# A recommendation model on one core: one gathered column of seven tiles moves from GpSimd to row-by-row DMAs of SyncE

## The reference

```python
h = relu(dense @ dw1 + db1)
dense_emb = relu(h @ dw2 + db2)
sparse_emb = emb_tables[f_ids, sparse_idx]
emb = concatenate([dense_emb[:, None, :], sparse_emb], axis=1)   # 27 vectors of 64
inter = einsum('bfd,bgd->bfg', emb, emb)
pairs = inter[:, iu0, iu1]                                       # 351 products
z = concatenate([emb.reshape(B, -1), pairs], axis=1)
z = relu(z @ ow1 + ob1); z = relu(z @ ow2 + ob2); z = relu(z @ ow3 + ob3)
return z @ ow4 + ob4
```

## Time and profile before

| what | value |
|---|---|
| median of 3 runs | 552.72 us (552.71 to 553.63) |
| profiled execution, its own time | 554.64 us |
| span of the profiled execution | 552.7 us |
| mean granted TensorE clock | 0.928 of full speed |
| busy: PE, POOL | 444.2 us (80%), 398.2 us (72%) |
| busy: ACT, DVE | 159.4 us (29%), 141.9 us (26%) |
| DMA traffic | 19.38 MB, mean 35 GB/s |

### The profile page before, as it was taken

One profiled execution on the slowest core, in us unless ns is written; L12 is line 12 of the kernel. 1 busy time (PEld: TensorE's weight loads), 2 busy tenths in 40 slices (PEclk: granted clock), 3 DMA queues, 4 the chain that ended last, 5 costly groups with the idle time before them and its releaser, 6 DMA issues.

```text
span 552.7 us, 5884 instructions
## 1 busy us (share of the span) xinstructions
PE 444.2 (80%) x2326; PEld 236.6 (43%) x2326; DVE 141.9 (26%) x225; ACT 159.4 (29%) x265; POOL 398.2 (72%) x420
## 2 busy tenths in 40 slices
PE   3757989585887979799685988979597899959978
PEld 1124553252534435354342534525253444525767
DVE  1003324031331223214032231413222123311412
ACT  1303334122232232324133232323333223332322
POOL 5777777777777777777777777777777777777720
PEclk9999999798898979979798998979989799997998
DMA  8633323233332323333232332324333232333310
GB/s 274 133 49 25 29 26 25 27 28 26 27 26 26 27 26 28 26 27 26 26 28 26 27 26 28 27 26 27 26 28 26 26 27 26 27 25 27 26 13 1
DMA packets 17166, 19.38 MB, mean 35 GB/s; under 512 B 7359, under 2 KB 8386, under 8 KB 17127
## 3 DMA queue, kind: packets, MB, share of 16 engines
q0 software_dynamic: 13312, 13.66, 30.5%
q1 hardware_dynamic: 3408, 5.02, 2.7%
q10 hardware_dynamic: 420, 0.34, 0.3%
HBM read 18.99 MB, written 0.01 MB: 34 GB/s over the span
## 4 chain that ended last, share of the span: by engine, by line
POOL 57%; issue 19%; PE 15%; DMA 6%; SPq 1%; ACT 1%; DVE 1%; POOLq 0%; DVEq 0%
POOL emb L212 57%; DMA w1p_sb<-ow_pairs_dram 5%; PE l_ps L588 5%; PE gram_ps L567 2%; PE tr_ps L616 2%; PE l_ps L656 1%; DMA emb<-table_dram,rows 1%; PE gram_ps L656 1%; PE tr_ps L540 1%; PE l_ps L594 1%; PE gram_ps L635 0%; SPq L189 0%; PE l_ps L581 0%; PE gram_ps L663 0%; PE l_ps L663 0%
## 5 line engine op out<-in xcount | busy, mean ns | idle before, releaser
L212 POOL DMA_INDIRECT emb<-table_dram,rows x416 | 398.0, 957 | 130.1 <-issue 125.6
L588 PE MATMUL l_ps<-w_sb,feat 128*128 128x512 f32 x390 | 204.3, 674 | 3.7 <-DVE feat L247 1.5
L588 PEld LDWEIGHTS l_ps<-w_sb,feat 128*128 128x128 f32 x390 | 81.8, 220 | 107.6 <-issue 89.8
L540 PE MATMUL tr_ps<-ident_sb,emb 128*128 128x128 f32 x208 | 39.3, 306 | 62.5 <-DMA emb<-table_dram,rows 61.4
L278 DVE COPY gram_c<-gram_ps 32x432 f32<-32x432 f32 x60 | 36.6, 610 | 138.8 <-PE gram_ps L567 138.4
L382 ACT COPY slots<-feat 64x512 f32<-64x512 f32 (+3 forms) x66 | 58.6, 888 | 45.6 <-DVE feat L247 43.6
L567 PEld LDWEIGHTS gram_ps<-slots 64*128 64x128 f32 x960 | 56.1, 188 | 26.8 <-issue 15.5
L567 PE MATMUL gram_ps<-slots 64*128 64x108 f32 x960 | 61.2, 277 | 6.7 <-DVE gram_c L278 6.7
L394 ACT COPY gram_c<-gram_ps 32x432 f32<-32x432 f32 x60 | 30.6, 509 | 122.4 <-PE gram_ps L567 122.0
L247 DVE COPY feat<-tr_ps 128x512 f32<-128x512 f32 (+1 forms) x32 | 15.7, 492 | 191.4 <-PE tr_ps L540 191.4
L540 PEld LDWEIGHTS tr_ps<-ident_sb,emb 128*128 128x128 f32 x208 | 26.1, 152 | 90.2 <-issue 88.7
(11 more groups left out here) (67 smaller groups left out, 174.9 us busy)
## 6 DMA issues: line engine op xcount, KB each, us to landing
emb<-table_dram,rows POOLq DMA_INDIRECT x416, 3.3
w_sb<-ow_dram SPq DMA_DIRECT2D x3, 1024.0 KB, 9.7
w1p_sb<-ow_pairs_dram SPq DMA_DIRECT2D x1, 708.0 KB
w_sb<-ow_dram SPq DMA_DIRECT2D x1, 512.0 KB, 21.8
w_sb<-ow_dram SPq DMA_DIRECT2D x1, 256.0 KB, 13.0
idx_raw<-idx_dram ACTq DMA_DIRECT2D x1, 208.0 KB, 2.6
w1d_sb<-ow_dram SPq DMA_DIRECT2D x1, 128.0 KB
w_sb<-ow_dram SPq DMA_DIRECT2D x1, 128.0 KB, 6.4
```

The lines of the kernel that those rows point to most:

```text
L212: pool.indirect_dma_start(out=emb[:, t % RING, c // 2, c % 2 * D:(c % 2 + 1) * D], out_offset=None, in_=table, in_offset=bass.IndirectOffs ...
L540: last = nc.tensor.transpose(tr_ps[:, n % 2, (k - a) * P:(k - a + 1) * P], emb[:, t % RING, k, :], ident_sb[:])
L588: nc.tensor.matmul(l1_ps[t % 2][:], feat[t % 2][:, n - 1, :], w1_sb[:, n - 1, :], start=False, stop=False)
```

## The change

In tiles 2, 4, 6, 8, 10, 12 and 15 the last column (the odd half of pair 12, the last one of the fourth group) is left out of POOL's loop. SP fetches it in its place: 128 DMAs a tile, one for each sample, each of one row of 256 bytes to one partition. The row numbers of these columns come in a small array of their own, one partition wide; ACT's queue loads it, three DVE instructions turn it into row numbers. SP reads 32 of them at a time into registers and issues 32 DMAs whose source address is worked out from a register. For a tile t of 4 or more it first waits until PE has transposed all of tile t-4. PE's wait ahead of the fourth group is lowered by 16 for each column that POOL no longer fetches, and a wait for the tile's own 128 row DMAs is added. SP's six stores of the result now stand behind all the row DMAs in its program.

```diff
+ROW_TILES = [2, 4, 6, 8, 10, 12, 15]
+ROWS_AT_ONCE = 32
...
+        row_raw = sb("row_raw", [1, len(ROW_TILES), P], I32)
+        row_wrap = sb("row_wrap", [1, len(ROW_TILES), P])
+        row_f = sb("row_f", [1, len(ROW_TILES), P])
+        row_of = sb("row_of", [1, len(ROW_TILES), P], I32)
...
             sp.dma_start(w4_sb[:], ow4).then_inc(w234_in, 16)
 
+            sp.wait_ge(row_step, 3)
+            for i, t in enumerate(ROW_TILES):
+                if t >= RING:
+                    sp.wait_ge(transposed, (t - RING + 1) * NG)
+                for p in range(0, P, ROWS_AT_ONCE):
+                    _, r = nc.values_load_multi_w_load_instructions(
+                        row_of[0:1, i, p:p + ROWS_AT_ONCE], engines=[mybir.EngineType.SP], min_val=0,
+                        max_val=NF * V - 1, skip_runtime_bounds_check_because="DVE clamps every row number")
+                    for k in range(ROWS_AT_ONCE):
+                        sp.dma_start(emb[p + k:p + k + 1, t % RING, NP - 1, D:2 * D],
+                                     table[bass.ds(r[k], 1), :]).then_inc(row_gathered[i], 16)
+
             for b, (a, e) in enumerate(BATCHES):
...
-                    for c in range(2 * a, 2 * b):
+                    for c in range(2 * a, 2 * b - (b == NP and t in ROW_TILES)):
                         pool.indirect_dma_start(
...
+            dve.wait_ge(row_idx_in, 16)
+            nc.vector.tensor_scalar(row_wrap[:], row_raw[:], 0.0, float(V), ALU.is_lt, ALU.mult).then_inc(row_step, 1)
+            dve.wait_ge(row_step, 1)
+            nc.vector.scalar_tensor_tensor(out=row_f[:], in0=row_raw[:], scalar=float(-V), in1=row_wrap[:],
+                                           op0=ALU.max, op1=ALU.add).then_inc(row_step, 1)
+            dve.wait_ge(row_step, 2)
+            nc.vector.tensor_scalar(row_of[:], row_f[:], float(V - 1), float((NF - 1) * V),
+                                    ALU.min, ALU.add).then_inc(row_step, 1)
...
             act.dma_start(idx_raw[:], idx).then_inc(idx_in, 16)
+            act.dma_start(row_raw[:], row_idx).then_inc(row_idx_in, 16)
             act.dma_start(bias_sb[:], biases).then_inc(dense_w_in, 16)
...
-                pe.wait_ge(gathered[t % RING][n], (t // RING + 1) * 32 * (b - a))
+                by_row = [u for u in ROW_TILES if u % RING == t % RING and u <= t and b == NP]
+                pe.wait_ge(gathered[t % RING][n], (t // RING + 1) * 32 * (b - a) - 16 * len(by_row))
+                if t in by_row:
+                    pe.wait_ge(row_gathered[ROW_TILES.index(t)], 16 * P)
```

More of the change, by code:

```diff
@@ L27, in bass_dlrm_kernel @@
     first: bass.AP,
+    row_idx: bass.AP,
     table: bass.AP,
@@ L119, in bass_dlrm_kernel @@
         gathered = [[sem(f"gathered{r}_{n}") for n in range(NG)] for r in range(RING)]
+        row_gathered = [sem(f"row_gathered{i}") for i in range(len(ROW_TILES))]
+        row_idx_in = sem("row_idx_in")
+        row_step = sem("row_step")
         out_stored = sem("out_stored")
@@ L783 @@
         "first_dram": _np.stack([base, idx[:, 0]], axis=1),
+        "row_idx_dram": _np.stack([idx[:, t, NF - 1] for t in ROW_TILES])[None],
         "table_dram": x["emb_tables"].reshape(NF * V, D),
```

## The result

The changed kernel takes **546.92 us** (median of 4 runs, 545.59 to 547.17). The kernel before took 553.17 us (4 runs, 552.71 to 553.96). The ratio is 0.9878, with a 95% interval of 0.9858 to 0.9899: 1.2% faster. The forecast was 545.1 us, 1.4% faster; against the 552.72 us that it started from that is a ratio of 0.9862, just inside the interval.

What follows compares the result with a forecast made beforehand. POOL's gathers, 1.262 us each, were taken as the bound until PE's tail; six fewer gave 552.7 - 7.6 = 545.1 us. The likeliest case spanned 543.5 to 547; the wider range reached up to 590.

Steps and rivals of the forecast that it cites:

- POOL as the bound, 1.262 us a gather, six that count: POOL's gather loop: six of seven dropped gathers lie ahead of the chain's last one, saving 7.6 us.
- The seventh: Tile 15's dropped gather, the very last of the kernel, where PE is not waiting: saves nothing.
- The cost of a row: SP's row loop: DMA 0.278 us with its pause, two short instructions, register load 0.075 a row; 0.45 us in all.
- The upper bound of 0.88: SP's cost per row at most 0.88 us, charging POOL's 0.30 us pause for the arithmetic and for each register loaded.
- the estimate of 588 us: Kernel time if SP's register loads cost about 200 ns a register, making a row 0.58 us.
- The margin: Tile 12, the strictest deadline: SP's rows are in time if a row costs under 0.513 us.
- rival A: SP's register work is dearer, 0.606 us a row, so tile 12's rows come late: 608 us; chance 0.22.
- Rival B: All SP rows pass one DMA engine, which becomes the bound at 0.60 us a row: 604 us; chance 0.09.
- Rival C: Gain taken back by row cost near 0.53, by PE, or by later-landing gathers: 552 us; chance 0.10.
- Rival D: The change also gains in tile 15, or POOL loses its longer gathers: 543.8 us; chance 0.03.
- The edits around it: DVE's three row-number instructions take 4 us, the new ACT DMA delays later loads at most 0.46 us; all hidden.

Runs made afterwards that it cites:

- Nobody: Changed kernel with the seven columns fetched by no engine, no SP rows and no PE wait for them: 546.14 us, against 546.61 for the changed kernel on that chip.
- both: Changed kernel, but POOL keeps all 416 gathers while SP also issues its 896 rows into a spare tile: 554.05 us, ratio 1.0004 to the kernel before.
- the kernel with tile 14: Changed kernel with SP taking the last column of tile 14 instead of tile 15: 545.04 us, ratio 0.9837 to the kernel before.
- the first four experiments: Columns unfetched, columns fetched twice, tile 14 for 15, every fourth row twice: 757.93, 926.06, 926.01, 980.96 us on a chip where the kernel before takes 766.73.
- both experiments: Changed kernel with 8 row numbers a register load instead of 32: 546.1 us; changed kernel with every fourth row issued twice: 577.36 us.
- the fixed rows: Changed kernel with SP's row addresses fixed in the program, without register loads or arithmetic: 546.5 us, ratio 0.987 to the kernel before.

## Why the prediction was right, point by point

**POOL as the bound, 1.262 us a gather, six that count: right.** 409 gathers from 4.52 to 518.77 make 1.260 each. The last gather of tile 14 starts at 487.37, where the prediction had it near 487, and PE's last group of that tile moved by 7.25 us, against 7.6. "Nobody" and "both" show from both sides that nothing else of the change has an effect that these runs resolve. The medians gained 6.25 us here and 6.93 on another chip; the missing microsecond is no larger than what the tail alone varies by, and was not traced further.

**The seventh is worth nothing: right**, by the kernel with tile 14. One sentence beside it was too strong: that the 26 gathers of tile 15 are beside the chain. PE came to group 2 of tile 15 just as it landed; in the changed kernel it waits 0.73 us for it, and in "both" 0.32. It changes no number of the sum, since these gathers moved with the rest, but the end hangs on POOL to 517.50 there. Only the last group of tile 15, the two columns behind those 24, was found landed in every kernel.

**The cost of a row: 0.482 us instead of 0.45.** The DMA was priced by the store of y at 0.228 and took 0.225. The load was priced by a round trip of 2.4 us and took 2.12, but not for that reason: it costs by the register, with a fixed part, and that the two came out alike for 32 registers is luck. The mis-sized term is the arithmetic. It is two short instructions, as chosen, but I counted their pauses only, not their own 37 and 29 ns: without loads and waits a row took (431.95 - 27 x 2.12 - 2.9)/896 = 0.415 us (the first of the 28 loads lies ahead of the 431.95), where 0.378 had been forecast. Part of the 66 ns came back, as the three pauses were nearer to 0.04 us than to 0.05.

The upper bound of 0.88 rested on a misreading: 0.30 us is not the longest pause of any sequencer in that profile, where PE stands 2.64 us on "issue" from 535.70 on. On the chip of the first four experiments a row cost 0.936, above the bound.

The Trainium skill ("Runtime: NRT & Kernel Launch", Instruction fetch mechanics) gives about 200 ns a register for loads from HBM. By these traces, with loads from SBUF, it is 55 ns a register and 0.34 us a load. The page's figure, carried over, gave the estimate of 588 us in the prediction, a loss in place of the gain.

**The margin: right.** 0.482 lies below 0.513. At 0.522 tile 12 is late and nothing is lost, and at 0.56 the time is 577: tile 12's arrival plus 110 to 113 us, in both experiments, was the rule behind rival A's line.

**Rival A** was the right one to fear, and did not occur on the chips where the changed kernel itself was timed; that it was not timed on one like that of the first four is luck. **Rival B** fell with the fixed rows. No view here separates the engines, so whether all rows share one of them is not shown; at 0.30 us a row it was not the limit. **Rival C**, that the gain is taken back, is excluded by the result, 0.9858 to 0.9899. "Both" excludes that part of it in which the rows disturb the gathers. **Rival D** fell with tile 14.

**The edits around it: nearly right.** The three DVE instructions took 0.61, 1.08 and 0.63 us against 4 us forecast, and were hidden; so was the later w1p wait, now over at 33.89 instead of 33.36. The new DMA on ACT's queue put off the next one by 0.55 us, from 1.20 to 1.75, where 0.46 had been called the most. What was charged at nothing and is not quite: POOL begins at 4.52 instead of 4.07, because the first table part lands later. It is the best candidate for the difference between 7.6 and the 7.25 us that tile 14 moved. In "nobody" POOL begins at 4.13, in the changed kernel on that chip at 4.80, and the medians are 0.47 us apart; with four runs each that is too small to be told from noise.

## What to carry to other kernels

Where a software gather is the bound at a fixed price per instruction, an idle hardware queue can take over whole columns row by row, if its price per row is known and the tightest deadline is worked out tile by tile, with the slack that the consumer has later. Take off those gathers that lie ahead of the last one in the chain: at the same count, tile 14 was worth 1.6 us more than tile 15. And a scheme of thousands of small sequencer instructions rests on a sequencer that keeps its pace: measure it on several chips before it is trusted, since with a margin of 0.03 us a row it has little else to stand on.

## What the hardware showed that was not expected

- A register load of 8 values from SBUF took 782 ns, of 32 values 2.12 us.
- One chip of the four that the experiments met stalled short instructions on SP for up to 1.4 us, held PE up too, and left POOL's gathers alone (948 ns in the mean).
- The same 374 matmuls at the end took 22.32 us at a granted clock of 0.99 and 25.23 at 0.86. Which of the two an execution gets was not tied to the change.
- In all seven kernels with register-addressed rows that were traced on the other chips the first load of 26 KB took 2.8 to 3.1 us to land, with 29 to 33 packets in instruction queue q14. In the kernel before, in "nobody" (8 packets each) and with fixed rows (15 packets) it took 2.4 to 2.5. The longer program seems to be paid for at the start; by which path was not tried.
- A DMA of one row issued at 10 us stood 12.5 us, while the first-layer weights were under way on the same queue.
